# Softmax attention stage of a five-stage block: one DMA for the peaks' row, another order on ScalarE

## The chip, the cores and the metric

One core of a Trainium2 chip runs the whole program. The metric is the device time in microseconds of one execution, 2583.53 us as the median of 3 runs (2583.38 to 2583.6).

The engines: TensorE (PE; its weight loads are PEld in the profile) multiplies into PSUM, VectorE (DVE), ScalarE (ACT) and GpSimd (POOL) work beside it, SyncE (SP) only issues DMAs. Each runs its own instructions in order, and they meet at semaphores.

## The reference, cut to what matters

The program computes two blocks of attention and experts. The change is in the first attention alone. It works on 64 batches of 64 channels by 256 positions; the kernel takes two batches at a time, so 128 rows by 256 and 32 tiles:

```python
q = split_heads(_proj(x, Wq, bq)); k = split_heads(_proj(c, Wk, bk)); v = split_heads(_proj(c, Wv, bv))
q = _apply_rotary(q_emb, q); k = _apply_rotary(k_emb, k)          # 8 heads of 8 channels per batch
scores = jnp.einsum('bhtc,bhsc->bhts', q, k) / math.sqrt(K_CH)    # 256 x 256 per head
p_attn = jax.nn.softmax(scores, axis=-1)
out = jnp.einsum('bhts,bhsc->bhtc', p_attn, v)
out = out.transpose(0, 1, 3, 2).reshape(b, N_HEADS * K_CH, t_t)
return _proj(out, Wo, bo)
...
x = x + jnp.tanh(g_xattn[0]) * _L0_xattn_ref(_layernorm(x, axis=-1), ctx_2048, ...)
x = x + jnp.tanh(g_ffn[0]) * _L0_ffn_ref(_layernorm(x, axis=-1), L0_ffn_router_w, ...)
```

The second line's router (top 2 of 8 experts per row) for the first 16 tiles is computed in this stage as well, as the tiles come out.

## The kernel before

`stage_softmax_attention` runs a software pipeline of steps i = -5 to 34, the same loop on every engine; one tile n passes through some nine steps. 16 heads of a tile are handled as 8 pairs k of two.

Scores are computed twice. First TensorE makes p_a (L816) for tile i+1 or i+2, and VectorE takes each score row's maximum into `top` (`maxima`, L735), two instructions a pair. In the middle of step i-1 TensorE transposes `top` for tile i into p_x (L877), ScalarE evicts it as `peak` (L664), 16 rows by 256, and SyncE writes it by four DMAs (L543) into row 31 of each 32-row group of the operand `rep`. There it is a 32nd row of the contraction, against -1, so that the second score matmul p_b (L809) comes out with the peak subtracted, and ScalarE's `exp(i, k)` (L630) can take the exponential of it straight into `prob`. `both(i, k)` on TensorE issues p_b of tile i and p_a of a later tile in turns, for two heads h; it waits for `exp(i, k-1)` and for the maxima of the pair before, as p_a and p_b have one buffer per h. `both(i, 0)` also waits for the peaks' row (peak_in, L796).

`values(i, g)` (L830) multiplies prob with the values, whose extra columns of ones give the softmax sums; ScalarE evicts these as o_raw (`keep`, L637). When the four groups of tile i-1 are out (`keep(i-1, 3)`, in the first half of step i), GpSimd issues eight DMAs (L592) that pack values and sums by rows. VectorE ends step i with the reciprocal of the sums (L782). GpSimd multiplies (`on`, L607), TensorE projects out (L894), ScalarE evicts y (L700) and GpSimd adds the input (`xo`, L576).

The start of the pipeline: VectorE's statistics, GpSimd's `rstd` (L582), VectorE's `low` (L762), ScalarE's normalised row `xn` (L655), TensorE's projections (L846, L847), the rotation on VectorE (L721) and GpSimd (`roped`, L600), the split into two parts on ScalarE (L688) and GpSimd (L602), and 12 DMAs on SyncE that replicate them into `rep` (`fill_rows`, L504).

The router, for tiles 0 to 15: VectorE's `spread` of xo of tile i-4 and GpSimd's `root` (L167) early in step i, VectorE's `centre` (L173) late in it, ScalarE's `scale`, which writes the normalised router row (L184) and counts row_ready, after the last exponential of step i. TensorE turns that row at the end of step i+1 (L193), ScalarE evicts it (`keep_turned`, L201), and a step later come the scores (L211, evicted by `keep_scores`, L219, between `exp(i, 3)` and `exp(i, 4)`). `root` has one buffer for its result, so it waits until ScalarE has written the row of the tile before:

```python
    def root(self, pool, g):
        pool.wait_ge(self.var_ready, g + 1)
        past(pool, self.row_ready, self.GRP * g)
```

On GpSimd the order of a step is: xo, rstd, root, the eight packing DMAs, roped, second part, on. On SyncE: zero-fill of a later stage's buffer (768 KB, L527), fill_rows, store of xo, the peaks' DMAs, and every fourth step two loads of 512 KB (L518). On ScalarE, before the change: exponentials 0 to 7 with the o_raw evictions between them; xn, peak and values' eviction (L670) after exponential 5; after exponential 7 the router row, the turned row, the first part, and y.

Of the kernel before, what the change touches and what calls it, by code (L numbers as in the profile page):

```python
# [12 lines left out]
fp32 = mybir.dt.float32  # L13
# [398 lines left out]
def stage_softmax_attention(nc, x_in, x_out, ctx, c):  # L412
# [15 lines left out]
    with st:  # L428
# [77 lines left out]
        with nc.Block() as block:  # L506
            @block.sync
            def _(sp):
# [16 lines left out]
                for i in every:  # L525
                    if 0 <= i < len(blanks):
                        sp.dma_start(blanks[i].rearrange("(p r) d -> p (r d)", p=PART), blank[:]).then_inc(cleared[int(i >= CLEARS[0])], 16)  # L527
                    n = i + 3
                    if live(n):
                        sp.wait_ge(lo_ready, n + 1)  # L530
                        sp.wait_ge(hi_ready, n + 1)
                        sp.wait_ge(rep_init, min(n + 1, 4))
                        past(sp, b_ready, 2 * PAIRS * (n - 3))
                        fill_rows(sp, n, range(4 if n else 2))
                    if live(i - 3):
                        sp.wait_ge(xo_ready, i - 2)
                        sp.dma_start(x_out[i - 3], xo[:, (i - 3) % KEEP, :]).then_inc(stored[(i - 3) % KEEP], 16)
                    n = i + 1
                    if live(n):
                        sp.wait_ge(peak_ready, n + 1)  # L540
                        for j in range(4):
                            at = 32 * j + SPLIT
                            sp.dma_start(rep[at:at + 1, n % 4, :, 0:T].bitcast(fp32), peak[4 * j:4 * j + 4, n % 2, :].bitcast(fp32)  # L543
                                         ).then_inc(peak_in[n % 2], 16)
                    if (i + 9) % LOAD == 0 and 2 <= (i + 9) // LOAD < TILES // LOAD:
                        load((i + 9) // LOAD)
                    if i == 8:
                        held.load(sp)
                    if 0 <= i - 9 < held.RAWS:
                        held.load_raw(sp, c["L0_ffn_gate_proj"], c["L0_ffn_up_proj"], i - 9, i - 8)  # L550
# [64 lines left out]
            def _(act):  # L615
# [10 lines left out]
                def exp(i, k):  # L626
                    for h in range(2 if live(i) else 0):
                        act.wait_ge(b_ready, 2 * (PAIRS * i + k) + h + 1)
                        past(act, pv_done, GROUPS * i + k // 2 - 1)
                        act.activation(prob[:, k % 4, h, :], p_b[:, 2 * T * h:2 * T * (h + 1)], ACT.Exp).then_inc(prob_ready, 1)  # L630
# [8 lines left out]
                for i in every:  # L639
# [3 lines left out]
                    exp(i, 2)  # L643
                    keep(i - 1, 3)
                    exp(i, 3)
                    if routed(i - 6):
                        route.keep_scores(act, i - 6, 1, p_x[0][:, T:T + 8])
                    exp(i, 4)
                    keep(i, 0)
                    exp(i, 5)  # L650
                    n = i + 5
                    if live(n):
                        act.wait_ge(low_ready, n + 1)
                        past(act, qkrot_ready, n - 1)
                        act.activation(xn[:, n % 2, :], xt[:, n % RING, :], ACT.Identity, bias=low[:], scale=rstd[:]  # L655
                                       ).then_inc(xn_ready, 1)
                    if n in (0, 1, 2):
                        begin(n + 1)
                    n = i + 1
                    if live(n) or live(i + 3):  # L660
                        act.wait_ge(v_ready, i + 4)
                    if live(n):
                        past(act, peak_in[n % 2], 64 * (n // 2))
                        act.activation(peak[0:HEADS, n % 2, :], p_x[0][0:HEADS, T:2 * T], ACT.Copy).then_inc(peak_ready, 1)  # L664
                    n = i + 3
                    if live(n):
                        if n == 0:
                            act.wait_ge(zeroed, 5)
                        past(act, pv_done, GROUPS * (n - 3))
                        act.activation(vaug[:, n % 4, :, :, 0:KC].rearrange("p c h k -> p (c h) k"),  # L670
                                       p_x[0][:, 0:T].rearrange("p (n k) -> p n k", k=KC), ACT.Copy).then_inc(vaug_ready, 1)
                    exp(i, 6)
                    keep(i, 1)
                    exp(i, 7)
                    if routed(i - 4):
                        route.scale(act, i - 4, lambda t: xo[:, t % KEEP, :])
                    if routed(i - 5):
                        route.keep_turned(act, i - 5, p_x[0][:, 0:T], turned[:])
                    if i == RANK:
# [10 lines left out]
                    if n == 0:  # L690
                        act.wait_ge(lo_ready, 1)
                        act.wait_ge(hi_ready, 1)
                        fill_rows(act, 0, (2, 3))
                    t = i - 2
                    if live(t):
                        act.wait_ge(wo_ready, t + 1)
                        if t == 0:
                            act.wait_ge(shift_ready, 1)
                        past(act, xo_ready, t - 1)
                        act.activation(y[:, t % 2, :], p_x[1][:, 0:T], ACT.Identity, bias=shift[:], scale=gate[:]  # L700
                                       ).then_inc(y_ready, 1)

            @block.vector
            def _(dve):
# [80 lines left out]
            def _(pe):  # L785
# [5 lines left out]
                def both(i, k):  # L791
# [1 line left out]

                    n, m = (i + 1, k + 4) if k < 4 else (i + 2, k - 4)
                    if live(i) and k == 0:
                        pe.wait_ge(peak_in[i % 2], 64 * (i // 2 + 1))  # L796
                    if live(n) and m == 0:
                        pe.wait_ge(rep_in[n % 4], REP * (n // 4 + 1))
                    for h in range(2):
# [1845 lines left out]
```

## Time and profile before

| what | value |
|---|---|
| median of 3 runs | 2583.53 us (2583.38 to 2583.6) |
| the profiled execution | 2571.76 us |
| its span, first to last instruction | 2569.9 us |
| mean granted TensorE clock | 0.926 |
| PE, PEld, DVE busy | 86%, 65%, 71% of the span |
| ACT, POOL busy | 45%, 43% |
| the attention stage | about 58 to 640 us, 32 steps |

All rows come from this one profiled execution. Times are us from the start of the span; a duration is of one instruction or, with x2 and more behind it, of the group. In a timeline the bracket tells how long the engine was idle before the instruction and what ended that. The granted clock is a share of 2.4 GHz. A DMA that SyncE or GpSimd issues lands later than its row; the landing is seen where an instruction waits for it. In "who waited for whom" a stall is put down to what came last.

### The profile page before, as it was taken

The numbers are of one execution on the slowest core, as the hardware profiler recorded it, in microseconds if no ns is written. First come the engines' busy times: TensorE is split into PE (matmuls) and PEld (weight loads), VectorE is DVE, ScalarE is ACT, GpSimd is POOL, SyncE is SP. The second block draws the span as 40 slices with busy tenths as digits, with TensorE's granted clock in tenths as the row PEclk, the third lists the DMA queues.
The fourth block names the chain that finished last, engine by engine and source line by source line (L and its number), as shares of the span: only waits on it lengthen the run. The fifth ranks groups of instructions, "written<-read, shape, count | busy, mean of one in ns | idle before, by whom it ended". The sixth has DMA issues, their size and how long they took to land. (4 is left out here: it accounts for less than half of the span.)

```text
span 2569.9 us, 60412 instructions
## 1 busy us (share of the span) xinstructions
PE 2199.1 (86%) x20880; PEld 1669.5 (65%) x20880; DVE 1835.5 (71%) x3965; ACT 1154.2 (45%) x2509; POOL 1104.7 (43%) x1111
## 2 busy tenths in 40 slices
PE   6889888886878799993899998999988699999990
PEld 4555555543766577762677777777766577888880
DVE  4888988872557787765878878878787374545754
ACT  2677767664534233323444444444333264333330
POOL 3454555565154500002555445455487600334736
PEclk9888989975899899997999999999999799999995
DMA  5455554442469523212332332322334382445854
GB/s 115 108 134 139 149 142 133 118 137 76 126 198 296 150 88 103 77 38 53 82 88 56 83 84 62 84 73 69 79 99 115 123 266 83 139 142 183 265 170 147
DMA packets 250435, 313.10 MB, mean 122 GB/s; under 512 B 45216, under 2 KB 202912, under 8 KB 250144
## 3 DMA queue, kind: packets, MB, share of 16 engines
q1 hardware_dynamic: 189168, 219.11, 30.7%
q0 software_dynamic: 26624, 58.79, 8.2%
q10 hardware_dynamic: 34352, 31.34, 3.6%
q8 instruction: 180, 2.95, 0.5%
q14 instruction: 111, 0.91, 0.1%
HBM read 122.40 MB, written 102.24 MB: 87 GB/s over the span
## 5 line engine op out<-in xcount | busy, mean ns | idle before, releaser
L2126 POOL TENSOR_TENSOR ca_qk<-ca_qk,ca_q_swap 128x512 f32<-128x512 f32 x160 | 248.9, 1556 | 366.6 <-DVE ca_q_swap L2304 366.1
L735 DVE TENSOR_REDUCE soft_top<-soft_pa 128x2 fp32r<-128x512 f32 x512 | 327.9, 683 | 83.0 <-PE soft_pa L816 80.2
L630 ACT ACTIVATE soft_prob<-soft_pb 128x512 f32<-128x512 f32 x512 | 286.1, 594 | 171.3 <-PE soft_pb L809 169.5
L809 PE MATMUL soft_pb<-soft_rep 32*128 32x256 f32 x1024 | 207.3, 359 | 53.2 <-DVE soft_top L735 27.6
L809 PEld LDWEIGHTS soft_pb<-soft_rep 32*128 32x128 f32 x1024 | 135.4, 211 | 170.3 <-issue 73.5
L816 PE MATMUL soft_pa<-soft_rep 31*128 31x256 f32 x1024 | 217.1, 366 | 5.9 <-DVE soft_top L735 3.5
L1459 PE MATMUL moe_py<-moe_w_d,moe_at 128*128 x788 | 212.7, 385 | 1.4 <-issue 0.8
L1440 PE MATMUL moe_pgu<-moe_w_hi,moe_xt_hi 128*128 x472 | 192.8, 408 | 22.7 <-DVE moe_xt_lo L1357 13.0
L2396 PE MATMUL ca_py<-ca_w_hi,ca_ot_hi 128*128 128x256 f32 x512 | 156.7, 306 | 38.3 <-DVE ca_ot_lo L2325 38.0
L1363 DVE TENSOR_TENSOR moe_act_f<-moe_silu,moe_pgu 128x256 f32<-128x256 f32 (+1 forms) x236 | 88.6, 375 | 131.5 <-ACT moe_silu L1258 131.2
L2304 DVE TENSOR_TENSOR ca_q_swap<-ca_q_swap,ca_sin_q 128x512 f32<-128x512 f32 x128 | 117.2, 916 | 82.0 <-DMA ca_q_swap<-ca_q_f 81.7
L1258 ACT ACTIVATE moe_silu<-moe_pgu 128x256 f32<-128x256 f32 (+1 forms) x236 | 82.4, 349 | 200.0 <-PE moe_pgu L1440 198.2
L1440 PE MATMUL moe_pgu<-moe_w_hi,moe_xt_lo 128*128 x472 | 171.1, 362 | 0.0
L1440 PE MATMUL moe_pgu<-moe_w_lo,moe_xt_hi 128*128 x472 | 170.7, 362 | 0.0
L830 PE MATMUL soft_po<-soft_prob,soft_vaug 128*32 128x256 f32 x2048 | 163.8, 446 | 0.0
L2188 ACT ACTIVATE ca_ot_hi<-ca_po 128x512 fp32r<-128x512 f32 x128 | 69.6, 595 | 209.7 <-PE ca_po L2494 209.7
L2396 PE MATMUL ca_pp<-ca_ht_hi,ca_w_hi 128*128 128x512 f32 x312 | 138.1, 443 | 22.8 <-ACT ca_q_f L2174 19.4
L1179 POOL DMA_INDIRECT moe_yg<-moe_ys_rows,moe_held x112 | 115.0, 1027 | 86.7 <-DVE moe_ys L1370 37.5
L1357 DVE TENSOR_TENSOR moe_xt_lo<-moe_pt,moe_xt_hi 128x256 fp32r<-128x256 f32 x236 | 99.5, 422 | 71.5 <-ACT moe_xt_hi L1253 70.2
L2396 PE MATMUL ca_py<-ca_w_lo,ca_ot_hi 128*128 128x256 f32 x512 | 150.3, 294 | 0.0
L2396 PE MATMUL ca_py<-ca_w_hi,ca_ot_lo 128*128 128x256 f32 x512 | 150.2, 293 | 0.0
L364 POOL DMA_INDIRECT moe_rows<-moe_x_new,moe_held x80 | 78.1, 976 | 163.3 <-DVE moe_ys L1370 91.5
(377 smaller groups left out, 6252.7 us busy)
## 6 DMA issues: line engine op xcount, KB each, us to landing
ca_q_swap<-ca_q_f SPq DMA_DIRECT2D x640, 64.0 KB
moe_xs<-moe_rows SPq DMA_DIRECT2D x236, 128.0 KB
soft_rep<-soft_parts SPq DMA_DIRECT2D x378, 64.0 KB
moe_rows<-soft_blank SPq DMA_DIRECT2D x27, 768.0 KB
moe_ys_rows<-moe_ys ACTq DMA_DIRECT2D x134, 128.0 KB, 1.7
moe_ys<-moe_ys ACTq DMA_DIRECT2D x102, 128.0 KB, 2.6
moe_xd<-scratch SPq DMA_DIRECT2D x64, 128.0 KB, 2.7
ca_vs<-ca_v SPq DMA_DIRECT2D x32, 256.0 KB, 3.8
```

Of the source, the lines that this page charges most:

```text
L630: act.activation(prob[:, k % 4, h, :], p_b[:, 2 * T * h:2 * T * (h + 1)], ACT.Exp).then_inc(prob_ready, 1)
L735: dve.tensor_reduce(heads[:, j, :, g], p_a[:, 2 * T * h:2 * T * (h + 1)].rearrange("p (c s) -> p c s", c=HALF), AX, ALU.max).then_inc(a_do ...
L809: mm = pe.matmul(p_b[:, out], rep[of, i % 4, g, at:at + PART], rep[of, i % 4, g, 0:T], start=True, stop=True)
L816: mm = pe.matmul(p_a[:, out], rep[of, n % 4, g, at:at + PART], rep[of, n % 4, g, T:2 * T], start=True, stop=True)
L830: mm = pe.matmul(p_o[g % 2][32 * j:32 * j + 32, 0:T], vaug[:, i % 4, sc, 4 * g + j, :], prob[:, (2 * g + j // 2) % 4, j % 2, sc * T:(sc + ...
L1179: pool.indirect_dma_start(out=yg[:, t % HELD, k, :], out_offset=None, in_=ys_rows[h], in_offset=bass.IndirectOffsetOnAxis(ap=slot_id[:, t, ...
L1357: dve.tensor_tensor(xt_lo[:, b % 2, :, :], p_t[b % 2][:, 0:DIM].rearrange("p (k t) -> p k t", k=KC), xt_hi[:, b % 2, :, :].bitcast(fp32), ...
L1440: mm = pe.matmul(p_gu[b % 2][:, 0:W2], x[:, b % 2, k, :], w, start=(n == 0), stop=(n == 3 * KC - 1))
L1459: mm = pe.matmul(p_y[b % 2][:, 0:DIM], at[:, b % 2, m, :], w_d[:, bass.ds(e, 1), m, :].rearrange("p a d -> p (a d)"), start=(m == 0), stop ...
L2126: pool.tensor_tensor(qk[:, u % 2, m, :], qk[:, u % 2, m, :], q_swap[:, p % 2, :], ALU.add).then_inc(qk_ready, 1)
L2304: dve.tensor_tensor(out.rearrange("p (b s) -> p b s", s=SEQ), src.rearrange("p (b s) -> p b s", s=SEQ), tab[int(m == RQ)][:].unsqueeze(1). ...
L2396: mm = pe.matmul(out, x, y, start=start and n == 0, stop=stop and n == len(todo) - 1)
```

## The change

Four edits, all in `stage_softmax_attention`. SyncE writes the peaks' row by one DMA with 16 rows of 1 KB into partitions 31, 63, 95 and 127, in place of four with four rows each; the waits count 16 instead of 64. On ScalarE the eviction of peaks and values goes ahead of xn. The eviction of y of tile i-2 moves from the end of step i to just before `exp(i, 7)`. The router row of tile i-4, which stood after `exp(i, 7)`, is now written in the next step, between `exp(i, 3)` and `exp(i, 4)`, for tile i-5.

```diff
--- before.py
+++ after.py
@@ -538,10 +538,8 @@
                     n = i + 1
                     if live(n):
                         sp.wait_ge(peak_ready, n + 1)
-                        for j in range(4):
-                            at = 32 * j + SPLIT
-                            sp.dma_start(rep[at:at + 1, n % 4, :, 0:T].bitcast(fp32), peak[4 * j:4 * j + 4, n % 2, :].bitcast(fp32)
-                                         ).then_inc(peak_in[n % 2], 16)
+                        sp.dma_start(rep[SPLIT:PART:32, n % 4, :, 0:T].bitcast(fp32), peak[0:HEADS, n % 2, :].bitcast(fp32)
+                                     ).then_inc(peak_in[n % 2], 16)
                     if (i + 9) % LOAD == 0 and 2 <= (i + 9) // LOAD < TILES // LOAD:
                         load((i + 9) // LOAD)
                     if i == 8:
@@ -643,24 +641,21 @@
                     exp(i, 2)
                     keep(i - 1, 3)
                     exp(i, 3)
+                    if routed(i - 5):
+                        route.scale(act, i - 5, lambda t: xo[:, t % KEEP, :])
                     if routed(i - 6):
                         route.keep_scores(act, i - 6, 1, p_x[0][:, T:T + 8])
                     exp(i, 4)
                     keep(i, 0)
                     exp(i, 5)
                     n = i + 5
-                    if live(n):
-                        act.wait_ge(low_ready, n + 1)
-                        past(act, qkrot_ready, n - 1)
-                        act.activation(xn[:, n % 2, :], xt[:, n % RING, :], ACT.Identity, bias=low[:], scale=rstd[:]
-                                       ).then_inc(xn_ready, 1)
                     if n in (0, 1, 2):
                         begin(n + 1)
                     n = i + 1
                     if live(n) or live(i + 3):
                         act.wait_ge(v_ready, i + 4)
                     if live(n):
-                        past(act, peak_in[n % 2], 64 * (n // 2))
+                        past(act, peak_in[n % 2], 16 * (n // 2))
                         act.activation(peak[0:HEADS, n % 2, :], p_x[0][0:HEADS, T:2 * T], ACT.Copy).then_inc(peak_ready, 1)
                     n = i + 3
                     if live(n):
@@ -669,11 +664,23 @@
                         past(act, pv_done, GROUPS * (n - 3))
                         act.activation(vaug[:, n % 4, :, :, 0:KC].rearrange("p c h k -> p (c h) k"),
                                        p_x[0][:, 0:T].rearrange("p (n k) -> p n k", k=KC), ACT.Copy).then_inc(vaug_ready, 1)
+                    n = i + 5
+                    if live(n):
+                        act.wait_ge(low_ready, n + 1)
+                        past(act, qkrot_ready, n - 1)
+                        act.activation(xn[:, n % 2, :], xt[:, n % RING, :], ACT.Identity, bias=low[:], scale=rstd[:]
+                                       ).then_inc(xn_ready, 1)
                     exp(i, 6)
                     keep(i, 1)
+                    t = i - 2
+                    if live(t):
+                        act.wait_ge(wo_ready, t + 1)
+                        if t == 0:
+                            act.wait_ge(shift_ready, 1)
+                        past(act, xo_ready, t - 1)
+                        act.activation(y[:, t % 2, :], p_x[1][:, 0:T], ACT.Identity, bias=shift[:], scale=gate[:]
+                                       ).then_inc(y_ready, 1)
                     exp(i, 7)
-                    if routed(i - 4):
-                        route.scale(act, i - 4, lambda t: xo[:, t % KEEP, :])
                     if routed(i - 5):
                         route.keep_turned(act, i - 5, p_x[0][:, 0:T], turned[:])
                     if i == RANK:
@@ -691,14 +698,6 @@
                         act.wait_ge(lo_ready, 1)
                         act.wait_ge(hi_ready, 1)
                         fill_rows(act, 0, (2, 3))
-                    t = i - 2
-                    if live(t):
-                        act.wait_ge(wo_ready, t + 1)
-                        if t == 0:
-                            act.wait_ge(shift_ready, 1)
-                        past(act, xo_ready, t - 1)
-                        act.activation(y[:, t % 2, :], p_x[1][:, 0:T], ACT.Identity, bias=shift[:], scale=gate[:]
-                                       ).then_inc(y_ready, 1)
 
             @block.vector
             def _(dve):
@@ -793,7 +792,7 @@
 
                     n, m = (i + 1, k + 4) if k < 4 else (i + 2, k - 4)
                     if live(i) and k == 0:
-                        pe.wait_ge(peak_in[i % 2], 64 * (i // 2 + 1))
+                        pe.wait_ge(peak_in[i % 2], 16 * (i // 2 + 1))
                     if live(n) and m == 0:
                         pe.wait_ge(rep_in[n % 4], REP * (n // 4 + 1))
                     for h in range(2):
```

## Rows read from the trace of the kernel before

**Rows 1.** Busy time by engine of one stretch: us, PE, PEld, DVE, ACT, POOL, PEclk, DMA.
```profile
300.00:400.00 100.00, 89.55 (x850) 54.10 (x849) 89.61 (x195) 71.34 (x157) 52.65 (x79) 0.93 0.50 134
```

**Rows 2.** Who waited for whom, TensorE then VectorE, 58 to 625: total, times, longest.
```profile
PE soft_pb L809 <- DVE soft_top L735: 27.6, 42, 3.7
PE soft_pb L809 <- DMA soft_rep<-soft_peak: 13.9, 21, 2.7
PE soft_px L846 <- ACT soft_y L700: 3.9, 13, 0.6
...
DVE soft_rsum L782 <- DMA soft_sums<-soft_o_raw: 25.7, 6, 15.7
```

**Rows 3.** Timeline of TensorE, step boundary at 335: start, us, instruction, idle before it.
```profile
335.22 0.38 PE L809 MATMUL soft_pb<-soft_rep 32*128 32x256 f32 x1 [0.25 <-DMA soft_rep<-soft_peak]
```

**Rows 4.** Timeline of VectorE, 319 to 337.
```profile
319.89 1.22 DVE L735 TENSOR_REDUCE soft_top<-soft_pa 128x2 fp32r<-128x512 f32 x2
...
334.26 1.74 DVE L782 RECIPROCAL soft_rsum<-soft_sums 128x256 f32<-128x256 f32 x1
335.92 1.22 DVE L735 TENSOR_REDUCE soft_top<-soft_pa 128x2 fp32r<-128x512 f32 x2
```

**Rows 5.** Timeline of SyncE (DMA issues), 320 to 337.
```profile
320.85 8.81 SPq L504 DMA_DIRECT2D soft_rep<-soft_parts  x12
...
331.54 2.52 SPq L543 DMA_DIRECT2D soft_rep<-soft_peak  x4
```

**Rows 6.** Timeline of ScalarE, 320 to 337.
```profile
326.22 1.09 ACT L630 ACTIVATE soft_prob<-soft_pb 128x512 f32<-128x512 f32 x2 [0.91 <-PE soft_pb L809]
...
327.88 1.09 ACT L630 ACTIVATE soft_prob<-soft_pb 128x512 f32<-128x512 f32 x2 [0.51 <-PE soft_pb L809]
...
330.67 0.59 ACT L655 ACTIVATE soft_xn<-soft_xt,soft_low,soft_rstd 128x256 f32<-128x256 f32 x1
331.16 0.36 ACT L664 ACTIVATE soft_peak<-soft_px 16x256 fp32r<-16x256 f32 x1
...
333.01 1.20 ACT L630 ACTIVATE soft_prob<-soft_pb 128x512 f32<-128x512 f32 x2
334.11 0.59 ACT L184 ACTIVATE soft_r_rows<-soft_xo,soft_r_shift,soft_r_rstd 128x256 f32<-128x256 f32 x1
...
335.38 0.56 ACT L700 ACTIVATE soft_y<-soft_px,soft_shift,soft_gate 128x256 f32<-128x256 f32 x1
```

**Rows 7.** Timeline of GpSimd, 320 to 337.
```profile
322.68 0.54 POOL L167 TENSOR_TENSOR soft_r_rstd<-soft_r_var,soft_r_half_neg 128x1 f32<-128x1 f32 x1
325.61 0.62 POOL L592 DMA_DIRECT2D soft_packed<-soft_o_raw  x1 [2.39 <-ACT soft_o_raw L637]
...
329.38 0.59 POOL L592 DMA_DIRECT2D soft_sums<-soft_o_raw  x1
329.93 1.34 POOL L600 TENSOR_TENSOR soft_roped<-soft_by_cos,soft_by_sin 128x512 f32<-128x512 f32 x1
```

**Rows 8.** GpSimd's last issue and VectorE's reciprocal, three times, from their timelines.
```profile
137.75 0.60 POOL L592 DMA_DIRECT2D soft_sums<-soft_o_raw  x1
...
144.90 1.75 DVE L782 RECIPROCAL soft_rsum<-soft_sums 128x256 f32<-128x256 f32 x1 [2.19 <-DMA soft_sums<-soft_o_raw]
...
545.99 0.62 POOL L592 DMA_DIRECT2D soft_sums<-soft_o_raw  x1
...
548.64 1.75 DVE L782 RECIPROCAL soft_rsum<-soft_sums 128x256 f32<-128x256 f32 x1
...
629.53 0.61 POOL L592 DMA_DIRECT2D soft_sums<-soft_o_raw  x1
...
631.82 1.75 DVE L782 RECIPROCAL soft_rsum<-soft_sums 128x256 f32<-128x256 f32 x1 [12.72 <-DMA soft_sums<-soft_o_raw]
```

**Rows 9.** TensorE at the first live boundary, and the stretch behind it by windows.
```profile
77.59 0.58 PE L809 MATMUL soft_pb<-soft_rep 32*128 32x256 f32 x1 [0.72 <-DMA soft_rep<-soft_peak]
...
77.00:84.00 7.00, 6.41 (x45) 3.64 (x46) 4.14 (x10) 2.59 (x6) 1.82 (x2) 0.53 0.44 165
```

## Prediction

> **What bounds the kernel now.** I read the mean busy shares of the attention stage first, then who waits for whom, then single steps in order of time. The change touches only this stage, about 58 to 640 us of the 2569.9 us span. Between 300 and 400 us VectorE is busy 89.6 of 100 us and TensorE 89.6 [rows 1], so neither has much to give. The waits the change aims at are small: TensorE waits 13.9 us in 21 places for the DMA of the peaks' row, and 3.9 us in 13 places for the output's eviction (`y`, L700) [rows 2]. That is 17.8 us, 0.7% of the span, and it would be the gain if nothing else came late at the same places.
>
> Something else does. Take the step boundary at 335 us. TensorE stalls 0.25 us for the peaks' DMA and starts its `both(i, 0)` at 335.22 [rows 3], so it could have started at 334.97. But VectorE has, without a gap, its last maxima, then the reciprocal of the sums (334.26 to 336.00), then the first maxima of the next step at 335.92 [rows 4]. `both(i, 1)` needs those maxima, so TensorE coming 0.25 us earlier only waits longer later. In 26 of the 31 boundaries between live steps the first maxima start right as the reciprocal ends. **VectorE sets the boundary**, with the reciprocal in it; later in the step control passes to TensorE and back. From one such start to the next is 16.03 us here (319.89 to 335.92) [rows 4], the shortest kind of step; the others run to about 17 to 22 us.
>
> **The change part by part.** Sums are made against the profiled execution (2569.9 us of span, 2571.76 with what lies around it). The median of the timed runs, 2583.53, is 11.8 us above it, and I carry the differences over to it unscaled.
>
> *One DMA for the peaks' row, peaks ahead of the normalised row.* SP issues four DMAs in 2.52 us [rows 5], 0.63 each; three go, so the last one is issued 1.89 us earlier. ScalarE evicts the peaks before `xn` rather than after: 0.49 us earlier by the starts at 330.67 and 331.16 [rows 6]. The row arrives about 2.4 us earlier. I take the landing after the issue as unchanged, since the bytes and the 1 KB rows are the same; if four rows per engine landed one after the other it would still be hidden by 2 us. The stall at the boundary goes entirely, but is worth something only where the reciprocal is not behind it: at the first live boundary, where TensorE starts at 77.59 after 0.72 us of that wait [rows 9] and there is no reciprocal yet (-0.7), and at the second (-0.1). `xn` comes later by two short evictions and is used only in the next step: nothing.
>
> The zero-fill (768 KB) and the loads behind the peaks on SP's queue start up to 2.4 us earlier too. That may clear the DMA engines sooner for the sums. VectorE waits for the sums for 25.7 us in six places [rows 2]; 15.7 and 5.8 of it lie at the stage's end, and the other four make 4.2, the longest of them 2.19 at 144.90 [rows 8]. Bounds 0 and -4.2; I take -1, as the fills that share the engines start no earlier.
>
> *`y` ahead of the last exponential.* It costs 0.56 us [rows 6] in front of `exp(i, 7)`, which is queued behind it with the copy of the parts. That exponential starts at 333.01, ends at 334.21, and would end at 334.77; TensorE needs it at 334.97 [rows 3, 6]. Covered by 0.2 us in the shortest step. What it saves, TensorE's 0.24 us wait for `y`, lies beside the reciprocal as well. Both nothing; with the cover gone it would cost at most 0.5 us a step.
>
> *Router rows mid-step.* On ScalarE the row (0.59 us) goes between `exp(i, 3)` and `exp(i, 4)`, before which ScalarE idles 0.51 us [rows 6]: at most 0.08 us late, and maxima come later there. But the row also moves from the end of step i-1 to the middle of step i, and **GpSimd waits for it**. `route.root` (L166 to 167) waits for row_ready up to the row before its own. Before the change that row was ready, and root ran at 322.68 [rows 7]. Now it must wait for `exp(i, 3)` to end (327.31) and the row (327.90), then 0.54 us: 328.44. Queued behind it on GpSimd are the eight DMAs of packed values and sums, whose first issue was 325.61 and last ends 329.97 [rows 7]. They move by 2.84 us, to 332.81, and the reciprocal waits for them. `roped` behind them (329.93, 1.34) would end at 334.1, before ScalarE copies it at about 334.9: covered by 0.7 us. Fifteen steps, i = 5 to 19, have this wait.
>
> How late the sums then are depends on their landing, which the trace shows at three distances: 1.68 us after the last issue where nothing else runs (630.14 to 631.82), at most 2.03 at 548.64, and 6.55 among loads and fills (138.35 to 144.90) [rows 8]. At 1.68 they land at 334.49 here, 0.23 us behind the present start of the reciprocal (334.26); at 2.03 it is 0.58; if the landing were not to shrink at all it would be the full 2.84. The longer steps have more room. Lower bound: 0.2 in five short steps, +1. Upper bound: 2.84 in 13 steps (in two GpSimd or TensorE is later anyway), +37. I take 2.03, five short steps and a little at a sixth: +3. The reason is that the 12 fills are issued from 320.85 to 329.66 [rows 5]: DMAs issued at 328.45 to 332.81 meet few of them.
>
> The Trainium skill ("DMA: Bandwidth & Descriptors", Queues, rings and completion order) says that each DMA engine alternates between the queues that have work for it, whoever issued it. The trace agrees, with 6.55 us beside other traffic against 1.68 alone; by that rule alone the cost would stay at the lower bound.
>
> *The clock.* Between 77 and 84 us, right behind the stall of 0.72 us, the granted clock was 0.53 [rows 9], mostly the lower level of 1.2 GHz. Three more such stretches begin at a boundary where TensorE waits for this DMA, and one a few us behind it. A step with one is about 1 us longer (77.59 to 94.56 is 16.97, against 16.03), one with two is 3.9 longer; together some 7 us. Stalls removed may take some of these with them, stalls made at the reciprocal may add others: bounds -7 and +7, I take -2.
>
> **Sum:** -0.8 - 1 + 3 - 2 = -0.8 us: 2582.7.
>
> **Rivals.** *A, the forecast: no change.* Both the gain and the new wait are small, 2577 to 2588.
> *B, the clock stays up.* The stalls at 77, 94 and 425 us go, their slow stretches too (-7), the sums come earlier (-4.2), the first boundaries give -0.8, GpSimd costs +1: -11.0, 2572.5. For it: slow stretches follow stalls. Against: at 425 and 145 the reciprocal still stalls TensorE.
> The Trainium skill ("TensorE: Matmul & The Clock Gate", HAM oscillation) tells of matmul loops that keep losing their clock to DMA waits. The trace agrees at 77 us (0.53) [rows 9]; the rule favours this rival.
> *C, slower: GpSimd's wait takes the reciprocal with it.* Place: `route.root` in 15 steps. Price: where the landing stays about 4 us or more, 2 us or more in most of them, some +15 and with extra slow clock +20: 2598 to 2604. It decides once the sums land over 1.45 us after their last issue in a 16 us step. For it: 6.55 us at 144.90; against: 1.68 and 2.03 where the issue came late.
> *D, the merged DMA doesn't come earlier*, as its rows are slower than four DMAs' were. Then the stalls stay and `root` still costs: 2587.
>
> **How the numbers follow.** A 0.46, B 0.25, C 0.24, D 0.05. About 0.2% (5.2 us) is what a measurement of this kernel can tell from no change. A lies within it but for its edges. B and the low edge of A are faster: 0.26. C and a part of D are slower: 0.28. Within: 0.46. The range takes in B and the lower part of C: 2571 to 2597.
>
> **What the profile would show.** Right: no wait for the peaks' DMA left at L809 but also no shorter boundary; `root` starting behind the router row, with GpSimd idle for it 15 times; first issues of packed values about 2.8 us later; reciprocals with a short DMA wait in the 16 us steps; periods of 16.0 to 16.6 us there. Wrong: reciprocals that wait 1 us or more in most of the 15 steps (C), fewer stretches at the lower clock (B), or `both(i, 1)` starting earlier although the reciprocal did not, which would mean that I took the wrong engine for the bound.

## The result, and the profile after the change

| what | before | after |
|---|---|---|
| median, 4 runs each | 2583.45 us (2581.75 to 2583.6) | 2607.21 us (2600.99 to 2620.62) |
| ratio, with its 95% interval | | 1.01 [1.0061, 1.014] |
| profiled execution, its span | 2571.76, 2569.9 us | 2607.49, 2605.7 us |
| granted clock | 0.926 | 0.914 |
| end of the attention stage | 637.3 us | 672.2 us |

The change is about 1% **slower**, beyond the range of the forecast (2571 to 2597 us). The spans differ by 35.8 us, and the stage's end by 34.9: all of it lies in the stage. That is more than the medians differ by (23.8), since the profiled execution of before was a quick one. Below, boundary i is the start of `both(i, 0)`. Boundary 5 comes 5.6 us *earlier* than before (145.6 to 140.0), the next 16 steps take 315.4 us in place of 278.7, and the ten after them 182.4 in place of 179.9. The 15 waits of `root` lie in those 16 steps.

Busy time by engine of three stretches of the changed kernel (columns as in [rows 1]):
```profile
300.00:400.00 100.00, 86.23 (x751) 51.70 (x750) 81.42 (x177) 62.98 (x141) 47.16 (x70) 0.82 0.48 122
162.00:172.00 10.00, 9.93 (x72) 5.50 (x69) 6.78 (x18) 4.24 (x10) 1.89 (x4) 0.50 0.53 85
172.00:180.00 8.00, 7.63 (x78) 4.70 (x78) 6.16 (x11) 7.67 (x18) 6.26 (x10) 0.99 0.47 137
```
Against [rows 1] VectorE does 8 us less work in 100 us and the granted clock is 0.82 in place of 0.93. From 162 to 172 us it is 0.50: all at 1.2 GHz, while TensorE is busy 9.93 of 10 us. Added up from the trace's record of the clock, 112.6 us of the 15 steps from i = 6 ran at the lower level, against 41.0 before (with the step of i = 5, 119.5 against 47.8).

Who waited for whom in the changed kernel, 58 to 645 us (line numbers are one or two lower than before's):
```profile
POOL soft_r_rstd L167 <- ACT soft_r_rows L184: 103.9, 15, 7.6
PE soft_pb L808 <- DVE soft_top L734: 57.1, 61, 4.7
DVE soft_rsum L781 <- DMA soft_sums<-soft_o_raw: 22.2, 11, 8.7
PE soft_pb L808 <- DMA soft_rep<-soft_peak: 2.3, 3, 1.2
```
The waits aimed at are nearly gone: 13.9 us in 21 places [rows 2] became 2.3 in 3, and the one for `y` no longer shows. In their place TensorE waits 57.1 us for maxima, against 27.6. GpSimd waits 103.9 us for the router row, in 15 places as forecast.

One step of the changed kernel, timelines of ScalarE, GpSimd, SyncE (with one row of two steps later), VectorE and TensorE:
```profile
170.32 0.60 ACT L184 ACTIVATE soft_r_rows<-soft_xo,soft_r_shift,soft_r_rstd 128x256 f32<-128x256 f32 x1
...
171.06 0.55 POOL L167 TENSOR_TENSOR soft_r_rstd<-soft_r_var,soft_r_half_neg 128x1 f32<-128x1 f32 x1 [7.59 <-ACT soft_r_rows L184]
171.65 0.62 POOL L590 DMA_DIRECT2D soft_packed<-soft_o_raw  x1
...
175.42 0.59 POOL L590 DMA_DIRECT2D soft_sums<-soft_o_raw  x1
175.97 1.33 POOL L598 TENSOR_TENSOR soft_roped<-soft_by_cos,soft_by_sin 128x512 f32<-128x512 f32 x1
...
174.81 0.56 SPq L541 DMA_DIRECT2D soft_rep<-soft_peak  x1
175.41 0.45 SPq L527 DMA_DIRECT2D moe_rows<-soft_blank  x1
...
217.33 0.43 SPq L527 DMA_DIRECT2D moe_rows<-soft_blank  x1
...
159.20 1.75 DVE L781 RECIPROCAL soft_rsum<-soft_sums 128x256 f32<-128x256 f32 x1 [1.04 <-DMA soft_sums<-soft_o_raw]
160.87 1.22 DVE L734 TENSOR_REDUCE soft_top<-soft_pa 128x2 fp32r<-128x512 f32 x2
...
175.43 1.29 DVE L734 TENSOR_REDUCE soft_top<-soft_pa 128x2 fp32r<-128x512 f32 x2 [0.68 <-PE soft_pa L815]
176.63 0.70 DVE L173 SCALAR_TENSOR_TENSOR soft_r_shift<-soft_r_mv,soft_r_rstd 128x1 f32<-128x1 f32 x1
...
179.58 1.75 DVE L781 RECIPROCAL soft_rsum<-soft_sums 128x256 f32<-128x256 f32 x1 [1.04 <-DMA soft_sums<-soft_o_raw]
...
161.65 0.35 PE L808 MATMUL soft_pb<-soft_rep 32*128 32x256 f32 x1 [1.78 <-DVE soft_top L734]
```
Read these steps as a **loop that feeds itself**. The reciprocal waits 1.04 us for the sums (159.20). The maxima queued behind it come late, so TensorE's `both(i, 1)` starts at 161.65 after 1.78 us of idleness. Behind that stall come 10 us at half the clock. With them `exp(i, 3)` is late, so the router row (170.32), so `root` (171.06), so the packing DMAs, the last of which is issued at 176.01. The 768 KB zero-fill starts at 175.41, ahead of that. The reciprocal gets its sums 3.57 us after the last issue, having waited 1.04 us again (179.58). Boundaries 6 to 9 lie 20.4 to 20.6 us apart, each step with one such slow stretch. Steps without a slow stretch, as from 219.60 to 236.12, take 16.5. Nine of the 15 boundaries behind a waiting `root` (i = 6 to 20) have a TensorE stall over 1.5 us at `both(i, 1)`, against one before, and behind each of the nine the clock is at the lower level for 8 to 10 of the next 12 us.

The loop doesn't run through all nine. It closes at i = 6, 7 and 8 and ends at 9: the packing is as late there (last issue ends at 216.96), but the zero-fill comes behind it, at 217.33, and the reciprocal doesn't wait. Later stalls have starts of their own. At 12, 16 and 20 loads of 1 MB follow the peaks' DMA; ahead of 12 and 16 the step was a short one of 16.5 to 16.7 us. At 10, 14 and 18 the reciprocal has no wait for sums at all, but VectorE has the router's choice ahead of it. Reciprocals that wait 1 us or more are thus six of the 15.

### The profile page after: what moved, and what is told of

Its sections match the earlier page's. It is cut to its first block and busy times, and to the rows that moved or that the text cites. A ratio compares the mean times of both kernels' runs of the same rounds, so it can differ in the third digit from the quotient of the medians.

```text
span 2605.7 us, 60316 instructions
## 1 busy us (share of the span) xinstructions
PE 2219.7 (85%) x20880; PEld 1677.2 (64%) x20880; DVE 1845.1 (71%) x3965; ACT 1148.8 (44%) x2509; POOL 1105.4 (42%) x1111
## 5 line engine op out<-in xcount | busy, mean ns | idle before, releaser
L808 PE MATMUL soft_pb<-soft_rep 32*128 32x256 f32 x1024 | 213.9, 373 | 70.1 <-DVE soft_top L734 57.1
L815 PE MATMUL soft_pa<-soft_rep 31*128 31x256 f32 x1024 | 223.3, 381 | 3.7 <-DVE soft_top L734 3.5
L829 PE MATMUL soft_po<-soft_prob,soft_vaug 128*32 128x256 f32 x2048 | 172.2, 465 | 0.0
```

Source lines behind the costliest of these rows:

```text
L808: mm = pe.matmul(p_b[:, out], rep[of, i % 4, g, at:at + PART], rep[of, i % 4, g, 0:T], start=True, stop=True)
L815: mm = pe.matmul(p_a[:, out], rep[of, n % 4, g, at:at + PART], rep[of, n % 4, g, T:2 * T], start=True, stop=True)
L829: mm = pe.matmul(p_o[g % 2][32 * j:32 * j + 32, 0:T], vaug[:, i % 4, sc, 4 * g + j, :], prob[:, (2 * g + j // 2) % 4, j % 2, sc * T:(sc + ...
```

## The experiments

Single runs of one kernel lie up to 19 us from their median, so the intervals are what is compared. The ratio of "after" is to 4 runs of the kernel before; the others are to the kernel before, run beside each: medians 2583.39, 2583.68, 2585.41, 2586.75 and 2581.15 us in five series, 23 to 35 runs each. "Late sums" is what the reciprocals of those 15 boundaries waited for the DMA, "stalls" at how many of them TensorE was idle over 1.5 us at `both(i, 1)`, "low clock" what the 15 steps from i = 6 ran at 1.2 GHz, each from one profiled execution. That one need not be typical: it was the slowest run of e3 (2589.71 us) and e9 (2599.48), the fastest of e7 (2599.71) and e15 (2596.36).

| kernel | median us (runs) | ratio, 95% | late sums | stalls | low clock |
|---|---|---|---|---|---|
| before, as profiled | 2583.45 (4) | | 0.3 us | 1 | 41 us |
| after | 2607.21 (4) | 1.01 [1.0061, 1.014] | 10.4 | 9 | 113 |
| e1_rows_only | 2591.50 (10) | 1.0029 [1.0009, 1.005] | 2.3 | 3 | 61 |
| e2_rows_back | 2580.26 (10) | 0.9991 [0.9969, 1.0013] | 0.2 | 2 | 68 |
| e3_root_behind | 2581.60 (10) | 0.9989 [0.9969, 1.001] | 2.7 | 3 | 61 |
| e4_one_dma | 2577.45 (10) | 0.9981 [0.9954, 1.0007] | 3.1 | 2 | 51 |
| e5_fill_late | 2610.64 (9) | 1.0108 [1.0079, 1.0136] | 9.7 | 7 | 101 |
| e6_four_dmas | 2591.08 (10) | 1.0041 [1.0014, 1.0067] | 1.4 | 3 | 82 |
| e7_rows_one_dma | 2606.43 (4) | 1.011 [1.0046, 1.0175] | 6.9 | 7 | 89 |
| e8_one_dma_fill | 2590.56 (10) | 1.0038 [1.001, 1.0066] | 6.2 | 2 | 55 |
| e9_hold | 2592.64 (10) | 1.0028 [1.0006, 1.005] | 1.5 | 3 | 68 |
| e10_dma_hold | 2578.26 (12) | 0.9981 [0.9957, 1.0004] | 4.5 | 0 | 58 |
| e11_scalar_only | 2580.98 (10) | 0.9988 [0.9961, 1.0015] | 3.4 | 1 | 65 |
| e12_one_dma_again | 2581.51 (12) | 0.9991 [0.9967, 1.0015] | 2.0 | 1 | 48 |
| e13_hold_centre | 2590.31 (12) | 1.0017 [0.9996, 1.0038] | 3.3 | 4 | 68 |
| e14_rows_centre | 2589.20 (12) | 1.0014 [0.9991, 1.0036] | 9.9 | 3 | 72 |
| e15_after_centre | 2605.47 (6) | 1.0072 [1.0048, 1.0096] | 17.1 | 10 | 92 |
| e16_before_centre | 2576.03 (12) | 0.9959 [0.994, 0.9979] | 3.3 | 0 | 51 |
| e17_centre_again | 2572.17 (12) | 0.997 [0.995, 0.9989] | 2.3 | 0 | 31 |
| e18_centre_one_dma | 2570.84 (12) | 0.997 [0.9946, 0.9994] | 1.6 | 0 | 48 |

The four kernels above 2600 us are the four with 7 to 10 stalls; all others have at most 4. Late sums alone don't sort them: e14 has 9.9 us of them and e8 6.2, at 2589 to 2591 us.

**Which edit costs.** My theory: GpSimd's wait in `root`. Four kernels: the move of the router row alone (e1); the changed kernel with the row put back (e2); the changed kernel with `root` behind the packing DMAs (e3); one DMA alone (e4).

```diff
 # e3_root_behind: GpSimd
-                    if routed(i - 4):
-                        route.root(pool, i - 4)
                     t = i - 1
...
                                                ).then_inc(pack_in[t % 2], 16)
+                    if routed(i - 4):
+                        route.root(pool, i - 4)
```


> The kernel before with one edit of the change alone: the router row between exp(i, 3) and exp(i, 4) of the next step. Theory G (GpSimd's root waits for the row, the packing DMAs behind it and the reciprocal come late, TensorE stalls at both(i, 1) and its clock falls): nearly all of the loss comes back, 2605 to 2620 us; root waits for the router row 15 times, some 100 us in total, the 15 steps are 19 to 21 us long. Rival S (ScalarE's own order: y ahead of exp(i, 7) makes the last exponential late): this edit alone does little, 2580 to 2590 us.

> The changed kernel with the router row back behind exp(i, 7), the three other edits kept. Theory G: the loss is gone, and the first five steps keep what they gained (TensorE starts both(5, 0) at 140.0 us in the changed kernel, 145.6 before), so 2570 to 2580 us. Rival S: y still stands ahead of exp(i, 7), so still over 2595 us.

> The changed kernel with GpSimd's root moved behind the eight packing DMAs of the same step; the router row stays mid-step, so ScalarE's order is that of the changed kernel. Theory G: root finds its row written and waits little, packing starts as before the change, 2570 to 2582 us. Rival R (the router row itself makes exp(i, 4) late, GpSimd's wait being beside the point): still over 2595 us.

> The kernel before with one edit alone: the peaks' row by one DMA. Theory P (the gain of the first steps comes from the peaks' row, since without that stall TensorE keeps its clock and the sums' DMAs meet less traffic): half or more of the 5.6 us by both(5, 0), 2574 to 2580 us. Rival N (the boundary belongs to the reciprocal, so that TensorE only waits longer later, as the prediction had it): 2581 to 2585 us.

Without the late `root` the changed kernel equals before (e2 0.9991, e3 0.9989), so the whole loss hangs on it. e3 keeps the router row mid-step: it is the place of the wait, ahead of the packing DMAs, that costs, not the row. But e1 alone loses only 0.29%, some 8 us of 24 (by the intervals 2 to 13 of 16 to 36). The other 16 come only together with another edit, though one DMA alone loses nothing (e4). Waits of e1_rows_only:

```profile
POOL soft_r_rstd L167 <- ACT soft_r_rows L184: 96.0, 15, 7.6
PE soft_pb L809 <- DVE soft_top L735: 38.1, 57, 3.4
PE soft_pb L809 <- DMA soft_rep<-soft_peak: 13.5, 25, 1.4
```
GpSimd waits about as long as in the changed kernel, yet TensorE's waits for maxima are 38.1 us, not 57.1. Its waits for the peaks' row are still there, though: both kinds together are 51.6 us against 59.4.

**Which edit makes it 24.** Theory: with the one DMA SyncE gets to the zero-fill, and every fourth step to loads of 1 MB, some 2 us earlier, and that is into the packing DMAs which `root` has made late. So: both edits alone (e7, before with the router row mid-step and the one DMA), the changed kernel with four DMAs (e6), and the zero-fill moved behind the wait for the parts, ahead of `fill_rows` (e5 from the changed kernel, e8 from e4).

```diff
 # e5_fill_late, e8_one_dma_fill: SyncE; zero() issues the zero-fill
-                    if 0 <= i < len(blanks):
-                        sp.dma_start(blanks[i]..., blank[:]).then_inc(...)
...
                         past(sp, b_ready, 2 * PAIRS * (n - 3))
+                        zero()
                         fill_rows(sp, n, range(4 if n else 2))
+                    else:
+                        zero()
```


> The changed kernel with one thing moved: SyncE issues the zero-fill of 768 KB (L525 there) not right behind the peaks' DMA but after its wait for the parts, just ahead of fill_rows. Theory Z (the peaks' row by one DMA lets the zero-fill start while GpSimd's late packing DMAs are still under way, so that the sums land 3.5 us after the last issue in place of 1.7, the reciprocal waits, TensorE stalls over 1.5 us and its clock falls): the sums land 1.6 to 2.2 us after the last issue, both(5, 0) to both(21, 0) falls from 315 to about 295 us as where the router row alone was moved, 2582 to 2592 us. Rival Y (y ahead of exp(i, 7), and the peaks ahead of xn, on ScalarE): unchanged, 2600 to 2612 us.

> The changed kernel with the peaks' row written by four DMAs again, ScalarE's order as in the changed kernel. Theory Z: the zero-fill starts 1.9 us later and mostly misses the packing, 2588 to 2597 us. Rival Y: 2600 to 2612 us.

> The kernel before with two edits: the router row mid-step and the peaks' row by one DMA; ScalarE's order of peaks, xn and y as before. Theory Z: together they bring back the whole loss, 2600 to 2612 us, though one alone gave +8 and the other -6. Rival Y: the sum of the two, 2583 to 2590 us.

> The kernel before with one DMA for the peaks' row and the zero-fill moved ahead of fill_rows, the router row as before. A version that may beat both kernels. Theory Z: packing is early here (some 8 us behind both(i, 0)), so the zero-fill had been out of its way; moved, it delays fill_rows by some 2 us and overlaps packing more: 2574 to 2584 us, no better than one DMA alone (2577).

e7 is as slow as the changed kernel, so the two edits make up the loss. e6 takes back most of the 16. e5 took nothing back, and its trace tells why: the stalls sit at i = 8, 12, 16 and 20, where the loads follow the peaks' DMA, with the sums 4.8 to 5.15 us after the last issue, while at the other boundaries they land after 1.6 to 2.4. But stalls of 2.1 to 2.6 us at i = 10, 14 and 18 stayed without any wait for sums. The later zero-fill also costs by itself: e8 stands 0.4% above before, and e4 doesn't. Why was not tried; I had chosen a poor way to move it, and e5 doesn't tell what the zero-fill's meeting with the packing is worth.

**Holding back the transfers.** The straight test lets SyncE wait, in steps 5 to 20, until the packing DMAs have landed before it goes on to loads and zero-fill.

```diff
 # e9_hold (from the changed kernel), e10_dma_hold (from e4): SyncE, behind the peaks' DMA
+                    if 5 <= i < 21:
+                        sp.wait_ge(pack_in[(i - 1) % 2], PACK * ((i - 1) // 2 + 1))
                     if (i + 9) % LOAD == 0 and 2 <= (i + 9) // LOAD < TILES // LOAD:
```


> The changed kernel with one wait added on SyncE in steps 5 to 20: behind the peaks' DMA and ahead of the loads and the zero-fill it waits until GpSimd's packing DMAs of the step have landed. Moving the zero-fill alone had left the 1 MB of loads in that place, and every fourth boundary still had sums that landed 4.9 us after the last issue. Theory Z2 (zero-fill and loads together, started early by the one DMA, run into the late packing): the sums land 1.6 to 1.8 us after the last issue in all 15 steps, stalls over 1.5 us fall from nine to the three behind the router's choice, 2586 to 2596 us, as with four DMAs (2591). Rival W (TensorE comes early to the boundary, waits for the maxima in one piece, and its clock falls whatever the DMAs do): 2600 us and more.

> The kernel before with one DMA for the peaks' row and the same wait on SyncE; the router row as before. With the packing early the wait should cost nothing, and the zero-fill and loads never meet it. Theory Z2: packing meets fill_rows here, not the zero-fill, so little changes against one DMA alone: 2573 to 2581 us. Rival: the wait delays the loads and fill_rows behind them, 2583 us and more.

> The kernel before with ScalarE's order of peaks, xn and y alone: peaks and values ahead of xn, y ahead of exp(i, 7); four DMAs, router rows as before. By the prediction the cover of 0.2 us behind y holds and both edits are worth nothing: 2580 to 2586 us. Rival Y (y makes the last exponential late where the cover is gone): 2588 us and more. Rival P (the peaks 0.5 us earlier take the 0.25 us stalls away): 2575 to 2580 us.

> The same kernel as one DMA alone (2577.5 us, ratio 0.9954 to 1.0007), with more rounds, to tell whether it beats the kernel before. Theory P (stalls of the first five steps gone, some 5.5 us by both(5, 0)): 2575 to 2580 us and a ratio clear of 1. Rival N: 2581 to 2585 us.

e9 falls to 1.0028, where e1 is, with 1.5 us of late sums in place of 10.4. The control e10 equals e4, so the wait gains nothing where the packing is early. This **shows** that the 16 us hang on what SyncE sends behind the peaks' DMA while the late packing is under way. The wait holds back loads, zero-fill and all that follows them at once, so their shares stay unknown. A step with loads in the changed kernel, its SyncE, GpSimd and VectorE:

```profile
348.73 0.56 SPq L541 DMA_DIRECT2D soft_rep<-soft_peak  x1
349.41 0.39 SPq L518 DMA_DIRECT2D soft_xt<-in_x  x1
...
349.98 0.59 POOL L590 DMA_DIRECT2D soft_sums<-soft_o_raw  x1
...
356.09 1.75 DVE L781 RECIPROCAL soft_rsum<-soft_sums 128x256 f32<-128x256 f32 x1 [3.00 <-DMA soft_sums<-soft_o_raw]
```
The same kind of step in e6_four_dmas:
```profile
270.16 2.52 SPq L543 DMA_DIRECT2D soft_rep<-soft_peak  x4
272.79 0.39 SPq L518 DMA_DIRECT2D soft_xt<-in_x  x1
...
271.42 0.60 POOL L592 DMA_DIRECT2D soft_sums<-soft_o_raw  x1
...
274.46 1.74 DVE L783 RECIPROCAL soft_rsum<-soft_sums 128x256 f32<-128x256 f32 x1
```
And in e9_hold:
```profile
342.03 0.56 SPq L541 DMA_DIRECT2D soft_rep<-soft_peak  x1
345.50 0.39 SPq L518 DMA_DIRECT2D soft_xt<-in_x  x1
...
343.28 0.59 POOL L592 DMA_DIRECT2D soft_sums<-soft_o_raw  x1
343.83 1.33 POOL L600 TENSOR_TENSOR soft_roped<-soft_by_cos,soft_by_sin 128x512 f32<-128x512 f32 x1
...
343.86 1.33 DVE L173 SCALAR_TENSOR_TENSOR soft_r_shift<-soft_r_mv,soft_r_rstd 128x1 f32<-128x1 f32 x1
345.11 1.28 DVE L736 TENSOR_REDUCE soft_top<-soft_pa 128x2 fp32r<-128x512 f32 x2
346.31 1.74 DVE L783 RECIPROCAL soft_rsum<-soft_sums 128x256 f32<-128x256 f32 x1
```
The first x-load starts 1.2 us ahead of the last packing issue's end in the changed kernel, and the reciprocal waits 3.00 us. In e6 it starts 0.8 us behind it, in e9 1.6 us behind, and the reciprocal doesn't wait. The four slow issues had been keeping SyncE's large transfers off.

e11 and e12 settle the harmless edits: peaks and `y` ahead on ScalarE are worth 0.9988 [0.9961, 1.0015], the one DMA alone 0.9981 and 0.9991, none of them apart from no change.

**What the other 8 us are.** The last fence shows something new. `centre` (L173), on 128x1, takes 1.33 us in place of 0.15 under GpSimd's `roped`, which the late packing has pushed onto it, and the last maxima of the step stand behind it. The spread of its duration (ns min/median/max), in e4_one_dma, after, e9_hold and e14_rows_centre:

```profile
L173 DVE SCALAR_TENSOR_TENSOR soft_r_shift<-soft_r_mv,soft_r_rstd x16: 149/150/1331, 137.8 to 406.0; 128x1 f32<-128x1 f32 x16
```
```profile
L173 DVE SCALAR_TENSOR_TENSOR soft_r_shift<-soft_r_mv,soft_r_rstd x16: 149/711/1343, 138.3 to 432.9; 128x1 f32<-128x1 f32 x16
```
```profile
L173 DVE SCALAR_TENSOR_TENSOR soft_r_shift<-soft_r_mv,soft_r_rstd x16: 150/1136/1340, 139.0 to 417.8; 128x1 f32<-128x1 f32 x16
```
```profile
L173 DVE SCALAR_TENSOR_TENSOR soft_r_shift<-soft_r_mv,soft_r_rstd x16: 149/150/153, 141.6 to 420.0; 128x1 f32<-128x1 f32 x16
```
Four kernels put it behind the maxima of pair 7: from e9 (e13), from e1 (e14), from the changed kernel (e15) and from before, as control (e16).

```diff
                     maxima(i, 6)
+                    maxima(i, 7)
                     if routed(i - 4):
                         route.centre(dve, i - 4)
-                    maxima(i, 7)
```


> e9_hold with one more edit: VectorE's `centre` (L173) stands behind the maxima of pair 7 in place of between those of pairs 6 and 7. Theory X: of the 8 us that e9_hold is above the kernel before, most is `centre`, which GpSimd's late `roped` stretches from 0.15 to 0.7 to 1.3 us (its 16 durations sum to 14.4 us in e9_hold against 3.6 before) while `both(i, 7)` waits for the maxima behind it. Then the sum over L173 drops below 6 us and the time comes to 2580 to 2587. Rival Y: `centre` is only where the lateness shows, the maxima are late for another reason, or the order costs the same at the step's end: it stays at 2589 to 2596.

> e1_rows_only (the router row mid-step alone, 2591.5) with `centre` behind the maxima of pair 7. Theory X: 2580 to 2587, as for e13_hold_centre. Rival Y: 2589 to 2594.

> The changed kernel with `centre` behind the maxima of pair 7. Theory X with the theory of late sums: both costs stand side by side, so it falls by the 5 to 8 us of `centre` and keeps the 16 us of late sums: 2598 to 2603. Should the stretched `centre` also have been what starts the late sums, by making the exponentials and so the router row late, it falls further, to 2582 to 2595. Rival Y: 2605 to 2612.

> Control: the kernel before with `centre` behind the maxima of pair 7, where `roped` has long ended. Theory X: `centre` takes 0.15 us at either place, no change: 2580 to 2587. If it is 5 us faster, the order of the two is worth something by itself, and what e13_hold_centre and e14_rows_centre gain is not the stretching.

The stretching of `centre` goes (16 durations sum to 15.5 us in e1 and 2.4 in e14), but the time hardly follows: 1.0014 against 1.0029, 1.0017 against 1.0028, 1.0072 against 1.01, each within the other's interval. By their medians all three lie where rival Y has them. By their ratios, laid on 2583.5 us, e15 (18.6 us more) lies where X has it, and e13 (2587.9) and e14 (2587.1) lie between the two. Worse for theory X, the control gained 0.41% by itself, with `centre` at 0.15 us in 15 of 16 steps before and in all of them after. That called for a repeat, and for the version the runs point to, the control with the one DMA:

> The same edit as e16_before_centre, once more, beside e18. e16_before_centre was the control and came out 0.41% faster (10.7 us), which no theory had foreseen: its wait for `root` is none and `centre` takes 0.15 us at either place. If the gain belongs to the order (the last maxima of a step 0.15 us earlier, fewer TensorE waits for them), the ratio is 0.994 to 0.998 again. If it was the spread of the runs, 0.998 to 1.002.

> e17_centre_again with the one DMA for the peaks' row. If both are worth what they showed alone (one DMA 2 to 6 us, the order up to 10), it is 2570 to 2576, the fastest of all. If the one DMA only gives back at late sums what it saves, as in e8_one_dma_fill and e10_dma_hold, it equals e17_centre_again within 2 us.

The order is worth 0.3% again (0.997 [0.995, 0.9989]). Against that control the move of the router row costs 1.0014 / 0.9959 = 1.0055, so **theory X falls**: the stretching of `centre` is real and at most a small part of the 8 us. They stay open. The low clock doesn't explain them as it stands: e1 has 61 us of it and e9 68, but e3 has 61 and e2 68 without a loss. What the traces offer, not tested: with `root` waiting the packing starts 11.0 (e9) to 11.7 us (e1) behind the boundary, against 7.4 before, and the sums land under 0.85 us ahead of the reciprocal at 13 of the 15 boundaries of e1 and 12 of e9, against 6 before, so little room is left.

And X was tested for `centre` alone. At i = 10, 14 and 18 VectorE has the router's choice (some 1.4 us) ahead of the reciprocal, and two of its instructions, L231 and L237, also take two inputs from SBUF. In e9_hold, VectorE, GpSimd and TensorE:
```profile
235.44 1.09 DVE L237 TENSOR_TENSOR soft_r_picked<-soft_r_left,soft_r_score 128x32 f32<-128x32 f32 x1
...
235.22 1.27 POOL L602 TENSOR_TENSOR soft_parts<-soft_roped,soft_parts 128x512 fp32r<-128x512 f32 x1 [2.86 <-ACT soft_parts L697]
...
238.89 0.35 PE L810 MATMUL soft_pb<-soft_rep 32*128 32x256 f32 x1 [2.48 <-DVE soft_top L736]
```
L237 takes 1.09 us in place of 0.19 here, and 0.78 to 1.60 in e13 and e14, right ahead of the reciprocal. Over the profiles of all 20 kernels one of the two is stretched (0.49 to 1.83 us) at 38 of these 60 boundaries, and at 36 of the 38 TensorE stalls over 1.5 us; at the other 22 it does so twice. e16 to e18 have neither the stretching nor a stall there. Yet e3 has both (in its slowest run) and loses nothing by its median, so this too is a lead and not the answer. Moving the choice behind the reciprocal would test it.

e18 is the fastest by median (2570.84 us) but not apart from e17, both ahead of both given kernels.

## Why the prediction was wrong, step by step

*What sets the boundary.* Right, and it carried further than I took it. VectorE's reciprocal and the first maxima behind it set `both(i, 1)`; that is where all nine TensorE stalls over 1.5 us of these steps lie in the changed kernel.

*The peaks' row, -0.8 us.* The mechanism was right (13.9 to 2.3 us of waits), its place not complete. I counted only the first two boundaries; boundary 5 came 5.6 us earlier, in e4 too. Boundary 2 alone came 2.9 us earlier (94.56 to 91.64), with 1.3 us of slow clock in the step ahead of it in place of 6.7. At boundaries 4 and 5 I had taken the DMA as covered by the reciprocal, whose own sums wait at 144.90 (2.19 us, [rows 8]) became 0.60 in e4. But it isn't kept: e4 and e12 end 2 to 5 us ahead of before, within the uncertainty.

*Earlier zero-fill and loads, -1 us, bounds 0 and -4.2.* **The step that failed.** I let the earlier start only clear the DMA engines for the sums, and shut out a loss without a reason from a row. In the same text I moved the packing 2.84 us later [rows 7] and the fill 2.4 us earlier [rows 5], and did not put the two together: the fill had begun behind the packing (in e1_rows_only the fill of the step with packing from 283.88 to 288.24 starts at 291.08), and now begins inside it. The two together measured +16 us (e1 against the changed kernel), and e9_hold took them back.

*The wait in `root`, +3 us, bounds +1 and +37.* Mechanism, place and count were right: 15 waits, and the sums' landing of 2.03 us that I took is 1.96 us on the mean in e1. Mis-sized by 5 us: alone it measured +8, of which no run shows how it comes about. I took the delay of the packing from one short step, 2.84 us, where it is 4.3 us on the mean in e1 and 5.7 in the changed kernel, as the router row follows `exp(i, 3)` and so moves with every delay. The reason I gave for a short landing, that few fills are left by then, holds for `fill_rows` and not for what stands behind the peaks on the same queue.

*The Trainium skill's rule* ("DMA: Bandwidth & Descriptors", Queues, rings and completion order), that each DMA engine alternates between queues with work, is in keeping with the 3.5 to 5.5 us of the sums beside the zero-fill and the loads against 1.7 without. Which of the engines' queues held them up no run shows.

*`y` and the normalised row, nothing.* Right: e11 is within no change.

*The clock, -2 us, bounds ±7.* Wrong sign and size. The stretches at 1.2 GHz in the 16 steps grew by 72 us against the quick execution of before, by some 50 against e11 or e3, and each short step of 16.5 us became one of some 20.4 with one. I had priced the clock as a term beside the others. At i = 6 to 8 it closes the loop, since a slow step makes the next packing late (13.4 us behind its boundary, against 10.1 in a step of 16.5 us).

*Sum and rivals.* 2582.7 forecast, 2607.2 measured. The case that happened is rival C, by its place and by its point of decision (landing over 1.45 us in a short step), with a price of 15 to 20 us where it was 24. Its own sign, reciprocals that wait 1 us or more in most of the 15 steps, did not show: six waited so. Nor was its point of decision a good one, as e1 has all 15 landings over 1.45 us and loses 8 us. And the range did not take in "the lower part of C", as I wrote: it ends at 2597, C begins at 2598. Rival D fell with e4: TensorE's wait for the peaks' row is 3.4 us there against 13.9. Rival B, the clock stays up, happened nowhere with a late `root`. C's chance of 0.24 rested on landings of one queue's traffic as it was, not as the change would leave it.

## What to carry to other kernels

When a change moves one engine's DMAs later and another's earlier, lay both on one time axis before either gets a price: the meeting can cost more than both parts (8 us alone and -2 to -5 alone, the latter not apart from nothing; 24 together). A cheap instruction that waits, put ahead of a batch of DMA issues, makes all of them wait; behind the batch (e3_root_behind) it cost nothing. Where a late step is followed by a slow clock and that makes the next step late, price the loop, not the first delay, and look in the trace for how many steps it lasts (three here).

## What the hardware showed that I had not expected

A 128x1 operation of VectorE with two inputs in SBUF (`centre`, 0.15 us) took up to 1.34 us when it fell under GpSimd's 128x512 `roped`, and ended with it: 343.86 + 1.33 against 343.83 + 1.33 in e9_hold. The 14 long ones of e1_rows_only (0.7 to 1.34 us) all ended so, whereas the maxima, which read PSUM, kept their 1.29 us beside it (175.43 to 176.72, under 175.97 to 177.30). The kernel before had it too: `low` (L762), the same operation, took 0.15 us as a rule and up to 1.87 under `roped`. The Trainium skill ("SBUF — State Buffer", SBUF: two separate sides) says that such an operation and GpSimd's hold their common port for a whole instruction each; the trace agrees.

The stalls at `both(i, 1)` that the lower clock follows are short: after 1.78 us of idleness TensorE ran the next 10 us at 0.50, though busy 9.93 of them. And a reordering that no theory here had expected anything of, `centre` behind the last maxima, gave 0.3 to 0.4%. It is the only edit that came out faster than no change, and why stays open (TensorE's waits for maxima are 26.8 us in e16 against 27.6).
